# Two graph layers over eight batches: the product of T written into the low half's place, its steps placed one by one, and the low halves of A taken on VectorE

## What is computed

```
h  = relu(layernorm(x))
T  = A * exp(leaky(sj[None, :] + si[:, None] + ab));  T = T / sum(T, axis=-1)
x  = x + relu(sum over k of Xk @ Wk[k] + bk[k])       X0 = h, X(k+1) = T @ Xk, k = 0, 1, 2
h  = relu(layernorm(x))
An = dh[:, None] * (A + I) * dh[None, :],  dh = 1 / sqrt(sum(A + I, axis=-1))
x  = x + relu((An @ h) @ kernel + bias)
```

## Time and profile before

| | us |
|---|---|
| median of 3 runs | 859.63 (859.32 to 862.04) |
| the profiled execution | 860.75 |
| its span, first to last instruction | 858.0 |
| mean granted TensorE clock | 0.996 |
| PE busy | 797.3 (93% of the span) |
| VectorE (DVE) busy | 641.2 (75%) |
| ScalarE (ACT) busy | 509.0 (59%) |
| GpSimd (POOL) busy | 300.3 (35%) |

### The profile page before, as it was taken

The page is one execution under the profiler, slowest core; times in us unless marked ns, Lnnn a source line. Parts: engine busy times, 40 slices in busy tenths (PEclk is TensorE's granted clock), DMA queues, the critical chain, the costliest instruction groups (busy, mean ns, idle before and its releaser), DMA issues.

```text
span 858.0 us, 15999 instructions
## 1 busy us (share of the span) xinstructions
PE 797.3 (93%) x6140; PEld 765.6 (89%) x6140; DVE 641.2 (75%) x1400; ACT 509.0 (59%) x997; POOL 300.3 (35%) x247
## 2 busy tenths in 40 slices
PE   4979999899989999899998999989998999989998
PEld 3869898899989999798998989989998999989998
DVE  4477697966978677985879759787687867787565
ACT  1597646766467564775647754576646756468232
POOL 1003234442263332631335323443325433163416
PEclk9998999999999999999999999999999999999999
DMA  5437242862347432674317734286243751256503
GB/s 184 172 123 221 87 135 68 254 219 92 107 141 245 158 124 70 200 237 166 129 37 216 252 104 136 62 251 228 66 132 119 234 201 46 91 176 202 190 23 99
DMA packets 65275, 128.70 MB, mean 150 GB/s; under 512 B 6320, under 2 KB 32304, under 8 KB 65200
## 3 DMA queue, kind: packets, MB, share of 16 engines
q1 hardware_dynamic: 54768, 93.86, 33.5%
q10 hardware_dynamic: 10432, 33.82, 13.3%
HBM read 119.28 MB, written 8.39 MB: 149 GB/s over the span
## 4 chain that ended last, share of the span: by engine, by line
PE 73%; DVE 15%; ACT 5%; issue 4%; POOL 1%; DMA 1%; SPq 0%; ACTq 0%; DVEq 0%
PE acc L984 17%; PE acc L986 16%; PE acc L985 16%; PE da L854 13%; PE db L854 6%; PE tp L846 3%; DVE a_raw L690 3%; DVE tg_e L647 3%; ACT t_hi L414 2%; DVE t_lo L651 2%; DVE z_tmp L702 2%; DVE o_tile L707 1%; POOL a_lo L311 1%; DVE ht_lo L608 1%; ACT tg_e L404 1%
## 5 line engine op out<-in xcount | busy, mean ns | idle before, releaser
L984 PE MATMUL acc<-g_hi,t_hi 128*128 128x256 f32 (+1 forms) x1024 | 293.1, 286 | 6.5 <-DVE g_tmp L665 5.2
L986 PE MATMUL acc<-g_hi,t_lo 128*128 128x256 f32 (+1 forms) x1024 | 290.1, 283 | 0.0
L985 PE MATMUL acc<-g_lo,t_hi 128*128 128x256 f32 x1024 | 288.9, 282 | 0.0
L311 POOL TENSOR_TENSOR a_lo<-a_raw,a_hi 128x512 fp32r<-128x512 f32 x128 | 186.3, 1474 | 177.3 <-ACT a_hi L455 175.7
L984 PEld LDWEIGHTS acc<-g_hi,t_hi 128*128 128x128 f32 x1024 | 194.2, 190 | 6.9 <-DVE g_tmp L665 5.5
L985 PEld LDWEIGHTS acc<-g_lo,t_hi 128*128 128x128 f32 x1024 | 194.6, 190 | 0.0
L986 PEld LDWEIGHTS acc<-g_hi,t_lo 128*128 128x128 f32 x1024 | 194.4, 190 | 0.0
L984 PE MATMUL acc<-g_hi,a_hi 128*128 128x256 f32 x512 | 147.3, 288 | 25.9 <-POOL a_lo L311 25.8
L985 PE MATMUL acc<-g_lo,a_hi 128*128 128x256 f32 x512 | 144.1, 281 | 0.0
L986 PE MATMUL acc<-g_hi,a_lo 128*128 128x256 f32 x512 | 143.9, 281 | 0.0
L404 ACT ACTIVATE tg_e<-si,sij 128x256 f32<-128x256 f32 x256 | 110.1, 502 | 25.1 <-DVE t_lo L651 25.1
(11 more groups left out here) (105 smaller groups left out, 1495.0 us busy)
## 6 DMA issues: line engine op xcount, KB each, us to landing
tg_a<-adj_t_dram ACTq DMA_DIRECT2D x64, 512.0 KB, 4.0
a_raw<-adj_dram SPq DMA_DIRECT2D x64, 512.0 KB, 4.1
a_raw<-adj_t_dram SPq DMA_DIRECT2D x64, 512.0 KB, 5.1
x_res<-x_dram SPq DMA_DIRECT2D x64, 128.0 KB, 3.5
out_dram<-o_tile SPq DMA_DIRECT2D x64, 128.0 KB, 3.2
h<-x_dram SPq DMA_DIRECT2D x7, 1024.0 KB, 5.5
h<-x_dram SPq DMA_DIRECT2D x4, 256.0 KB, 4.9
p<-wk_dram SPq DMA_DIRECT2D x1, 768.0 KB, 7.8
```

Source lines behind the costliest of these rows:

```text
L311: nc.gpsimd.tensor_tensor(a_half(a_lo, i, h), a_raw[:, i % RS, h * N // 2:(h + 1) * N // 2], a_half(a_hi, i, h).bitcast(F32), ALU.subtract ...
L984: nc.tensor.matmul(acc[:, s, 0:n], l_hi, r_hi, start=(jt == 0), stop=False)
L985: nc.tensor.matmul(acc[:, s, 0:D], l_hi, r_lo, start=False, stop=False)
L986: ins = nc.tensor.matmul(acc[:, s, 0:n], l_lo, r_hi, start=False, stop=(jt == NT - 1))
```

## The change

T's product no longer lands in `tg_e` but in the place of `t_lo` (a second name, `t_raw`, for the same bytes). High reads it there, and low subtracts in place. Units 0 and 1 of every batch but the first still go by `tg_e`. So leaky of unit u + 2 waits for the product of unit u, not for its low. The half steps and their tables go; each step has its own table (`SCORE_V`, `HIGH_V`, `PROD_V`, `LOW_V` in V, `LEAKY_Z`, `EXP_Z`, `HIGH_Z`, `PROD_Z`, `LOW_Z` in Z, and those with U). In the first batch, all four steps of T stand behind each tile of the dense stage, one unit for each tile. The diagonal of chunk 6 is added behind chunk 2 of Z (it was chunk 3), that of chunk 7 behind chunk 3 (it was 4). All `a_lo` halves are subtracted on VectorE (`a_low`), none on GpSimd. The first rounds of A (chunks 0 and 1) are placed behind tiles 2, 3, 6 and 7 of the dense stage.

```
+    SCORE_V = {-1: 1, 2: 2, 3: 3, 5: 4}
+    HIGH_V = {1: (0, 1), 5: (2,), 7: (3,)}
+    PROD_V = {0: 1, 3: 2, 5: 3}
+    LOW_V = {1: 0, 2: 1}
+    LEAKY_Z, EXP_Z = {0: 5, 4: 6, 6: 7}, {0: 5, 5: 6, 6: 7}
+    HIGH_Z, HIGH_U = {3: 4, 5: 5}, {0: 6, 1: 7}
+    PROD_Z, PROD_U = {2: 4, 5: 5, 7: 6}, {0: 7}
+    LOW_Z, LOW_U = {1: 3, 6: 4, 7: 5}, {1: 6, 2: 7}
+    BEFORE_U = 6
-    DIAG_Z = {0: 4, 1: 5, 3: 6, 4: 7}
+    DIAG_Z = {0: 4, 1: 5, 2: 6, 3: 7}
...
+        at = (nc.sbuf_base + 31) // 32 * 32
+        sb("t_lo_space", [P, NT, NT, P])
+        t_lo = nc.alloc_sbuf_tensor_at("t_lo", [P, NT, NT, P], F32R, offset=at)
+        t_raw = nc.alloc_sbuf_tensor_at("t_raw", [P, NT, NT, P], F32, offset=at)
...
+        def t_parts(b, u):
+            return tg_e[:, u % TS] if b > 0 and u < 2 else t_view(t_raw, u)
...
+            def leaky(b, u):
+                s = u % TS
+                if b == 0 and u >= TS or u >= 2 * TS:
+                    act.wait_ge(prod_ready, b * NU + u - TS + 1)
+                elif u >= TS:
+                    act.wait_ge(t_ready, b * NU + u - TS + 1)
...
             for t in range(NT):
                 dense0(0, t)
-                t_step(0, *HALVES[t + 1], False, first=True)
+                if 0 < t <= BEFORE_U:
+                    t_high(0, t - 1, False)
+                if t + 1 < NU:
+                    leaky(0, t + 1)
+                    exponent(0, t + 1)
...
+            def t_prod(b, u):
+                s = u % TS
+                if b > 0 and u >= 2:
+                    dve.wait_ge(acc_full, (b - 1) * PHASES + NT + 2 * (u // 2) + 2)
+                dve.wait_ge(e_ready, b * NU + u + 1)
+                dve.wait_ge(tg_loaded[s], 16 * (b * (NU // TS) + u // TS + 1))
+                nc.vector.tensor_tensor(t_parts(b, u), tg_a[:, s], tg_e[:, s], ALU.mult).then_inc(prod_ready, 1)
...
+            def a_low(b, i, h):
+                dve.wait_ge(a_hi_done[h], b * NT + i + 1)
+                nc.vector.tensor_tensor(a_half(a_lo, i, h), a_raw[:, i % RS, h * N // 2:(h + 1) * N // 2],
+                                        a_half(a_hi, i, h).bitcast(F32), ALU.subtract).then_inc(a_ready[h], 1)
...
                 for i in range(NT):
+                    if i > 1 and i in A_FIRST:
+                        a_low(b, *A_FIRST[i])
                     z_chunk(b, par, i)
+                    if i == 0:
+                        a_low(b, *A_FIRST[0])
+                    if i in LOW_Z and not last:
+                        t_low(b + 1, LOW_Z[i])
                     if i in DIAG_Z:
                         diag(b, DIAG_Z[i])
-                    if not last:
-                        for step in T_Z[i]:
-                            t_step(b + 1, *step)
+                    if i == 1:
+                        a_low(b, *A_FIRST[1])
+                    if i in A_THEN:
+                        a_low(b, *A_THEN[i])
+                    if i in PROD_Z and not last:
+                        t_prod(b + 1, PROD_Z[i])
```

More of the change, by code:

```diff
@@ new lines, in exponent, with t_high @@
+            def exponent(b, u):
+                act.wait_ge(leaky_done, b * NU + u + 1)
+                nc.scalar.activation(tg_e[:, u % TS], tg_e[:, u % TS], ACT.Exp).then_inc(e_ready, 1)
+            def t_high(b, u, last):
+                if b > 0 and u < 2:
+                    act.wait_ge(acc_full, (b - 1) * PHASES + NT + 2)
+                act.wait_ge(prod_ready, b * NU + u + 1)
+                nc.scalar.copy(t_view(t_hi, u), t_parts(b, u)).then_inc(t_hi_done, 1)
+                nxt = next_unit(b, u, last)
+                if nxt is not None:
+                    load_t_unit(act, *nxt)
@@ L435, in rows, with layer0_dense @@
+            def layer0_dense(b, after):
+                for t in range(NT):
+                    if t % 2 == 0 and t + 2 < NT:
+                        transposed_hi(t // 2 + 1, tp0_full, b, ht0_hi_done)
+                    dense0(b, t)
+                    if t % 2 == 0 and t > 0:
+                        si_copy(b, t // 2 - 1)
+                    after(t)
             def rows(b, t):
@@ L463, in batch, with after @@
                     nc.scalar.copy(g1_hi[:, i, :], g1_tmp[:, i % 2, :]).then_inc(g1_hi_done, 1)
-                    for step in T_U.get(i, ()):
-                        t_step(b, *step, last, first=True)
+                    if i in HIGH_U:
+                        t_high(b, HIGH_U[i], last)
                     for t in ROWS_U.get(i, ()):
                         rows(b, t)
-                def between(g):
-                    if g == NG - 1:
+                def after(t):
+                    if t == 2:
                         a_round(b, 0, 0)
+                    if t == 3:
                         a_round(b, 0, 1)
-                    if not last:
-                        for step in T_D.get(g, ()):
-                            t_step(b + 1, *step, False)
+                    if t == 4 and not last:
+                        leaky(b + 1, 0)
+                    if t == 5 and not last:
+                        exponent(b + 1, 0)
+                    if t == 6:
+                        a_round(b, 1, 0)
+                    if t == 7:
+                        a_round(b, 1, 1)
                 if not last:
-                    layer0_dense(b + 1, between)
+                    layer0_dense(b + 1, after)
                 else:
-                    between(NG - 1)
+                    for t in range(NT):
+                        after(t)
                 for i in range(-1, NT):
@@ L726, in batch, with after @@
                             norm0(1)
[L727 to L728 removed]
+                def after(t):
+                    if t == 0:
                         dve.wait_ge(rows_done, b * NT + NT)
                         nc.vector.tensor_scalar_add(row_a1[:, :], row_a[:, :], 1.0).then_inc(rows1_done, 1)
[L732 to L736 removed]
+                    if t == 1:
+                        diag(b, 0)
+                    if t == 3:
+                        a_low(b, 0, 0)
+                    if t == 4:
+                        a_low(b, 0, 1)
+                        diag(b, 1)
+                    if t == 5:
+                        diag(b, 2)
+                    if t == 6 and not last:
+                        t_prod(b + 1, 0)
+                    if t == 7:
+                        a_low(b, 1, 0)
+                        a_low(b, 1, 1)
+                        diag(b, 3)
                 if not last:
[L739 removed]
+                    layer0_dense(b + 1, 1 - par, after)
                 else:
[L741 to L746 removed]
+                    for t in range(NT):
+                        after(t)
                 for i in range(NT):
@@ L827, in _ @@
                 dense0(0, 0, t)
[L828 to L834 removed]
+                if t <= BEFORE_U:
+                    t_prod(0, t)
+                if 0 < t <= BEFORE_U:
+                    t_low(0, t - 1)
             for b in range(0, B - 3, 2):
```

217 lines of the change are left out of this document (62 added, 155 removed).

## The result

| | us |
|---|---|
| before, median of 4 runs | 859.72 (859.32 to 862.04) |
| after, median of 4 runs | **838.76** (838.61 to 840.16) |
| ratio, 95% interval | 0.9755 (0.9738 to 0.9772) |
| the profiled execution of after, and its span | 840.16, 838.4 |

A forecast was written before the change was run, and what follows sets the result against it. The prediction took TensorE, busy 93% of the span, as the bound, so only its gaps could give time. 860.75 - 22.8 (Z) + 3.6 (first batch) = 841.5 against the profiled execution, forecast 841 us, range 834 to 852.

The forecast's parts named there:

- The walk of Z: VectorE's queue followed through Z: TensorE loses 1.0 us a batch in place of 4.26, gaining 22.8 us over seven batches.
- The price of a half: An `a_lo` half on VectorE in Z: taken as 0.6 us from start to start, from a row at 0.683.
- Why these waits: TensorE's waits in Z: GpSimd takes 1.47 us per `a_lo` half and slows VectorE, whose diagonals take 1.39 instead of 0.28.
- Rival 4: Z keeps its 4.26 us loss because the place of the steps releases rounding, not late VectorE: 864 us; chance 0.03.
- Later batches, dense, V and U at nothing: Dense, V and U after the first batch: the moved work fits into idle time there and costs nothing.
- The first batch: Dense and U of batch one: ScalarE at 4.18 us a tile, U starting at 63.85, cost 3.6 us.
- rival 1: First dense stage loses clock: U's first chunk takes 5.3 us, not 2.85, dense may stretch some 2; 844 to 846; chance 0.15.
- the loads decide: Loads of chunks 6 and 7 in Z land late: 847 us at 5.1 each, 857 at 6.5; chance 0.15.
- rival 3: VectorE becomes the bound of Z if a half costs 1.47 us, turning point 1.0: about 900 us; chance 0.07.
- The sum: Whole kernel: 860.75 - 22.8 + 3.6 = 841.5 us against the profiled execution, forecast as 841.

The follow-up runs named there:

- l1_order: Changed kernel with two `l1_low` steps of VectorE moved one step earlier each, ahead of the L1 dense stage; 839.92 us, 0.9763 of the kernel before.
- diag_late: Changed kernel with the diagonals of chunks 6 and 7 back in their old places, one chunk later on VectorE; 842.36 us, 0.9789 of the kernel before.
- gp_bystander: Changed kernel plus a GpSimd subtraction of constants, awaited by nobody, where each `a_lo` half used to be; 889.41 us, 1.0350 of the kernel before.
- before_product: Kernel before with only T's product moved to `t_lo`'s place, old step order, halves on GpSimd; 857.73 us, 0.9979 of the kernel before.
- first_13: Changed kernel with 13 first-batch half steps of T before U, units 5 to 7 finished between U's chunks 0 to 3; 831.41 us, ratio 0.9677.
- first_13_stats: first_13 with the next batch's statistics moved from U into VectorE's idle stretches ahead of it; 832.43 us, 0.9685 of the kernel before.
- gp_halves: Changed kernel with all `a_lo` halves back on GpSimd in the old order; 844.22 us, 0.9829 of the kernel before.

## Why the prediction was right, and where it was not

- **The walk of Z** held in the sum. It left 1.0 us lost in each batch, and 4.26 - 3.58 leaves 0.7: seven batches gave 25.1 where the text had 22.8. The load of chunk 6 landed by the trace at 352.54, which is 353.67 on the clock of the kernel before (the L1 wait comes 1.13 earlier after the change); the walk had 353.1, and VectorE free at 352.0, which came out as 352.06. What the walk had too dear is the count of waits: it had one ahead of the second half of chunk 5 and one ahead of chunk 6 in every batch. The trace has one in three of the seven batches, ahead of chunk 6 (0.32 and 0.80 us) or of chunk 5 (0.44), and none of note in the other four. Which it is goes with the loads: in batch 2 VectorE waited 1.61 us for that of chunk 6, in batch 1 0.82 for it and 0.65 for that of chunk 7.
- **The price of a half**: 0.686 us, 0.6 from start to start, as taken.
- **"Why these waits"** is the step that was incomplete. It gave the whole wait to GpSimd, to its 1.47 us a half and to what it does to VectorE. The runs give 10.7 of 25.1 us to the halves and 14.2 to the placement of single steps (4.4 and 19.8 when taken in the other order), and with the new placement a slow GpSimd costs only 4.4. The walk counted the halves and the steps in their new places together, which is why the sum held all the same. Rival 4 would have been the fair place for this, in the form that both count; I had let it stand only as one against the other.
- **Later batches, dense, V and U at nothing**: right. TensorE's waits list none there; V and U take 23.8 to 24.0 us each, dense 19.0, as before within 0.3.
- **The first batch** was mis-sized: 3.6 in the text, 5.4 measured. The pace of a tile (4.17, the text had 4.18) and U's start (63.43, the text had 63.85) are right. U itself took 88.75 - 63.43 = 25.3 and not 23.2, since it began at the 1.2 GHz level (0.56 and 0.75 on the mean of the windows above). The 2.1 us are the first half of rival 1; its other half, a stretched dense stage, did not come, though the clock was 0.81 there: ScalarE set the pace, and TensorE had idle time to give. The rule of the Trainium skill, "TensorE: Matmul & The Clock Gate", section "A second HAM failure mode: psum-queue depth-cycling", that the clock can swing under frequent short idles, fits this trace: no wait inside the dense stage was above 1.8 us, and the clock fell in it (0.81 in the window from 43 to 52). Whether it is these idles or the single stop of 3.01 us ahead of U that had the clock low at U's start, the runs don't separate: in the changed kernel it is low through that stop, but in l1_order it was low from well before it (0.63 from 52 to 64).
- The term also had the wrong base. It was reckoned against a stop of 5.25 us, but the other parts of the change shorten that stop by themselves, to 3.71. Against the same kernel with the old first batch, the new one costs 7.4 by the head and 6.1 by the medians. That choice of the change was a loss, which the sum hid.
- **The other rivals**: the loads decide only in part. VectorE waits for that of chunk 6 in every batch, for 0.7 to 1.6 us, but when it doesn't (diag_late), another wait comes, of 0.82 us for TensorE in each batch. What the loads do set is the spread, some 0.9 us between the best and the worst Z. VectorE as the bound of Z (rival 3) is what gp_bystander looks like: 1032 ns a half, where the text had the turning point at 1.0, and it is slower than the kernel before.
- **The sum**: 858.0 - 25.1 + 5.4 + 0.1 (tail) = 838.4, the span. Two misses of 2.3 and 1.8 us had opposite signs, so the change of the span, 19.6, was nearer to the 19.2 of the text than either term: that is luck. The medians lie 21.0 apart, so 841 was 2.2 too high; that part is not in the terms, which are read from one execution each.

## What to carry to other kernels

When a change has three parts, time each alone and all but one: here the part with the striking rows (diagonals of 1.39 us beside GpSimd) was worth less than the dull one (the order of steps) whichever was taken first, a part that enables another showed nothing by itself, and a loss of 6 us in the first batch was hidden in the net gain. A wait that moves on under three placements in turn points to a sum of work on one engine: take work off it before you reorder again.

## What the runs showed of the hardware that I had not expected

- The clock doesn't follow from the length of one stop. In before_product TensorE stands still ahead of chunk 5 for 2.04 us in batch 0 and again in batch 2. Behind the first, which ended at 150.21, it ran at the 1.2 GHz level, behind the second, which ended at 354.73, at full clock (windows of PE, as above):

```profile
152.00:155.00 3.00, 3.00 (x16) 0.50 0.75 208
...
355.00:358.00 3.00, 2.81 (x24) 1.00 0.93 283
```

- The same in the first batch. Behind first_13's stop, which ended at 75.40, the window 76 to 80 has 0.69 (the stop was 2.51 us); behind the stop of 2.86 us in first_13_stats, ended at 80.25, the clock stayed at 1.00:

```profile
76.00:80.00 4.00, 4.00 (x26) 0.69 1.03 360
```

```profile
80.00:84.00 4.00, 3.75 (x18) 1.00 0.71 240
```

- Nor does it fall at the same place each time: l1_order has the first dense stage of the changed kernel unchanged, and was at full clock until 52 and at 0.63 from there to 64. The heads of the four runs with that first stage unchanged (after, gp_halves, gp_bystander, diag_late: 134.99 to 136.19) differ by 1.2 us.
- Subtractions that nobody reads, on an engine that was nearly idle, cost 6.2 us a batch in the changed kernel.
